# The second attention of a four-layer kernel, with scores made twice: by rows for the maximum, by columns less the maximum

## What is computed

```
# third layer, end of it:  y = ys + x * D_param ; x = x + y
def attention(x, ...):                       # fourth layer, 16 heads of 32
    kv_d = x @ kv_d_w ; q_d = x @ q_d_w
    k = concat(kv_d @ k_u_w, rope(x @ rope_k_w))
    q = concat(q_d @ q_u_w, rope(q_d @ rope_q_w))
    v = kv_d @ v_u_w
    scores = einsum('bqhd,bkhd->bhqk', q, k) / sqrt(32)
    scores = where(causal, scores, finfo.min)
    probs = softmax(scores)
    return einsum('bhqk,bkhd->bqhd', probs, v).reshape(b, s, H) @ o_w
```

## Time and profile before

| | us |
|---|---|
| median of 3 runs | 2087.54 |
| lowest and highest | 2086.83 and 2090.91 |
| the profiled execution | 2090.83 |
| its span, first to last instruction | 2089.1 |
| PE busy in the span | 1867.2 (89%) |
| DVE, ACT and POOL busy | 1369.4, 1000.2 and 801.1 |

### The profile page before, as it was taken

The page is one execution under the profiler, slowest core; times in us unless marked ns, Lnnn a source line. Parts: engine busy times, 40 slices in busy tenths (PEclk is TensorE's granted clock), DMA queues, the critical chain, the costliest instruction groups (busy, mean ns, idle before and its releaser), DMA issues. The chain is left out here.

```text
span 2089.1 us, 27327 instructions
## 1 busy us (share of the span) xinstructions
PE 1867.2 (89%) x9162; PEld 1222.5 (59%) x9162; DVE 1369.4 (66%) x2180; ACT 1000.2 (48%) x1743; POOL 801.1 (38%) x1073
## 2 busy tenths in 40 slices
PE   7978665899999899899999899899999999899795
PEld 3446444695448555596447656587447656588342
DVE  5765699475563699575654599676754599766311
ACT  1411675363422697363432598264242498365131
POOL 1146277442220277471220167381310157472301
PEclk9989855899999999999999999999999999999898
DMA  6336200000213175210213167210122158310693
GB/s 260 115 108 214 96 0 21 1 2 1 101 46 121 36 254 210 96 32 21 88 44 112 40 229 248 93 42 21 41 92 92 55 197 265 113 42 21 234 325 106
DMA packets 55065, 221.06 MB, mean 106 GB/s; under 512 B 6288, under 2 KB 6288, under 8 KB 46992
## 3 DMA queue, kind: packets, MB, share of 16 engines
q1 hardware_dynamic: 45776, 195.19, 26.9%
q0 software_dynamic: 5120, 16.78, 2.5%
q10 hardware_dynamic: 4032, 7.34, 1.0%
HBM read 179.70 MB, written 39.58 MB: 105 GB/s over the span
## 5 line engine op out<-in xcount | busy, mean ns | idle before, releaser
L2004 POOL TENSOR_TENSOR Y<-Y,HC 128x1024 f32<-128x1024 f32 x116 | 273.8, 2361 | 174.4 <-DVE HC L1378 173.7
L1367 DVE TENSOR_TENSOR_SCAN HS<-DA,ps 128x1024 f32<-128x1024 f32 x128 | 292.3, 2284 | 23.9 <-PE ps L761 13.5
L1748 ACT ACTIVATE DA<-DL,AB,AN 128x511 f32<-128x511 f32 x256 | 193.9, 807 | 14.7 <-DVE HS L1367 13.5
L544 PE MATMUL ps<-ring,XNT 128*128 128x512 f32 x384 | 176.1, 611 | 13.2 <-PEq L2036 9.1
L991 PE MATMUL ps<-ring,XBT 128*128 128x512 f32 x384 | 187.0, 593 | 0.2 <-ACT XBT L1427 0.2
L1867 ACT ACTIVATE PD<-ps,NMX 128x128 f32<-128x128 f32 (+3 forms) x256 | 134.9, 529 | 101.3 <-DVE NMX L1514 99.2
L1514 DVE TENSOR_REDUCE NMX<-ps 128x1 f32<-128x128 f32 (+3 forms) x256 | 124.3, 487 | 62.3 <-PE ps L829 61.9
L847 PE MATMUL ps<-V,PTD 128*128 128x33 f32 x1280 | 164.2, 262 | 0.0
L847 PEld LDWEIGHTS ps<-V,PTD 128*128 128x128 f32 x1280 | 162.6, 192 | 0.5 <-ACT PTD L869 0.5
L669 PE MATMUL ps<-XNH,tern 128*128 128x512 f32 x352 | 141.0, 401 | 10.8 <-DVE tern L1267 6.5
L1378 DVE TENSOR_TENSOR HC<-HS,ps 128x1024 f32<-128x1024 f32 x120 | 143.2, 1196 | 0.0
(11 more groups left out here) (251 smaller groups left out, 4015.4 us busy)
## 6 DMA issues: line engine op xcount, KB each, us to landing
ring<-experts_dram SPq DMA_DIRECT2D x48, 1024.0 KB, 5.2
tern<-tern_q SPq DMA_DIRECT2D x33, 768.0 KB, 4.3
ring<-experts_dram SPq DMA_DIRECT2D x48, 512.0 KB, 5.5
RAW<-tern_dram SPq DMA_DIRECT2D x22, 768.0 KB, 4.8
ring<-wqkv_dram SPq DMA_DIRECT2D x4, 3072.0 KB, 12.1
XB<-xg SPq DMA_DIRECT2D x42, 256.0 KB, 3.8
yg<-YB SPq DMA_DIRECT2D x42, 256.0 KB, 5.0
tern_q<-tern SPq DMA_DIRECT2D x11, 768.0 KB, 7.3
```

The costliest lines, as they stand in the source:

```text
L544: last = pe.matmul(ps[:, 2 + 3 * (i % 2) + part], XNT[:, k, tile(i)], wqkv[:, k, part * C:(part + 1) * C], start=(k == 0), stop=(k == NK - 1))
L1367: v.tensor_tensor_scan(HS[:, q].rearrange("p j t -> p (j t)"), DA[:, q].rearrange("p j t -> p (j t)"), ps[:, 2 * q:2 * q + 2].rearrange("p ...
L1748: s.activation(DA[:, u % 2, jj, 1:T], DL[:, j, 1:T], ACT.Exp, scale=AN[:, j * NS + n:j * NS + n + 1], bias=AB[:, j * NS + n:j * NS + n + 1 ...
L2004: p.tensor_tensor(y, y, HC[:, q], ALU.add).then_inc(c_y, 1)
```

## The change

Stage D is written anew in the manner of stage A. Per pair of heads there are three *units* (512, 512 and 256 columns for each of the two heads) and five kinds of PE work, in this order within a unit:

1. PV of an older pair (128 rows, 64 columns of the array),
2. masks: a bf16 identity times `mask_wide`, for the scores by rows (`pe_D_masks`),
3. spread: an f32r matrix of ones times DG, a diagonal matrix of the negative maxima, which puts minus the maximum of query q in column q of every partition (`pe_D_spread`),
4. rows: scores by rows, 32-row float32 matmuls added to the masks (`pe_D_rows`),
5. cols: scores by columns, 32-row float32 matmuls added to the spread (`pe_D_cols`).

So every score is made twice in float32: once by rows, from which DVE takes only the maximum (`v_D_max`, both heads in one instruction), and once by columns, less that maximum, which ACT exponentiates without a bias (`s_D_exp`). ACT also makes the diagonals, ten 128 x 128 products a pair (`s_D_diag`). POOL masks with `p_A_select` as in stage A. The loop has NP + 2 turns: turn t makes the rows of pair t, the columns of pair t - 1 and the PV of pair t - 2. PV writes always to bank 0, and PV of pair p waits for the division of pair p - 1 (`a_head`).

Gone are the stacks, the f32r split, QKS, the turning of PD, PTD and the turning of the heads; new are the 32 turns of QN into QT and KT at the front (`pe_qk` with "qk2"). The projection is made three quarters ahead (`pe_project_part`), the last quarter after the last division. On DVE a turn holds: the division of pair t - 3, the four maxima of pair t, then in turns 1 to 4 two `v_combine`, in turns 5 and 6 two `v_stats`, in turns 7 and 9 two `v_normalize`. On POOL all eight gathers go ahead of the first select.

At the end of stage C the last two HC are no longer added to Y; PE turns Y and HC one after the other into the same bank with float32 matmuls by the identity (32 matmuls for 16 transposes), and the experts' last matmuls are put around them. XS moves to where PT lies, so ACT waits in stage A, ahead of its second pair, for the scatter of XS. Buffers move accordingly.

The core of the diff:

```diff
-            for u in range(NU + 4):
-                if u < NU:
-                    ...
-                    pe.matmul(ps[:, bank, 0:(i + 1) * P], QKS[:, g % 2, hh, tile(i)],
-                              QKS[:, g % 2, GH + hh, 0:(i + 1) * P], start=True, stop=False, skip_group_check=True)
-                    pe.matmul(ps[:, bank, tile(i)], identb, mask_q, start=False, stop=True,
-                              skip_group_check=True).then_inc(d_scores, 1)
-                ...
+            for t in range(NP + 2):
+                rows, cols, heads = t < NP, 1 <= t <= NP, t >= 2
+                if t == NP + 1:
+                    pe.wait_ge(a_exp, 3 * (NP + t - 2) + 2)
+                    for i in range(2):
+                        pe_project_part(pe, i)
+                for unit in range(3):
+                    ...
+                    if heads:
+                        pe_D_pv(pe, t - 2, ((0,), (1,), (2, 3))[unit])
+                    if rows:
+                        pe_D_masks(pe, t, unit)
+                    if cols:
+                        pe_D_spread(pe, t - 1, unit)
+                    if rows:
+                        pe_D_rows(pe, t, unit)
+                    if cols:
+                        pe_D_cols(pe, t - 1, unit)
+        def pe_D_spread(pe, p, unit):
+            if unit == 0:
+                pe.wait_ge(d_diag, NT * (p + 1))
+                pe.wait_ge(d_max, max_count(p, 2))
+            ...
+        def pe_D_pv(pe, p, blocks):
+            if 0 in blocks:
+                if p == 0:
+                    pe.wait_ge(ones_a[1], 1)
+                pe.wait_ge(a_sel, NP + p + 1)
+                if p:
+                    pe.wait_ge(a_head, NP + p)
+            for kt in blocks:
+                last = pe_pv(pe, p, kt, 0)
+            if NT - 1 in blocks:
+                last.then_inc(a_pv, 1)
+            for t in range(NP + 3):
+                if t >= 3:
+                    v_pair(v, 1, t - 3)
+                if t < NP:
+                    for unit in range(3):
+                        v_D_max(v, t, unit)
+                if experts and 1 <= t <= NT:
+                    for n in (2 * t - 2, 2 * t - 1):
+                        v_combine(v, n)
+        def s_D_diag(s, p, unit):
+            for n, (i, _) in enumerate(D_ROWS[unit]):
+                s.wait_ge(d_max, NT * p + (0, 1, 3)[unit] + n + 1)
+                ...
+                for x in range(2):
+                    for block in ((i, i + 1) if i == NT - 1 else (i,)):
+                        ins = s.activation(DG[p % 2][:, x, tile(block)], ident, ACT.Copy,
+                                           scale=NMX[:, p % 2, i, x:x + 1])
-            v.tensor_tensor(Y[:, 2:4], Y[:, 2:4], HC[:, 1], ALU.add).then_inc(c_yt, 1)
-                    last = pe.transpose(ps[:, bank, tile(j)], Y[:, j, tile(i)], ident)
+                    pe.matmul(ps[:, bank, tile(j)], Y[:, j, tile(i)], ident, start=True, stop=False,
+                              skip_group_check=True)
+                    last = pe.matmul(ps[:, bank, tile(j)], HC[:, j // 2, j % 2, tile(i)], ident, start=False, stop=True,
+                                     skip_group_check=True)
```

## The result

The changed kernel takes 2320.1 us (median; 2316.6 to 2329.9), the kernel before 2089.2 us beside it: a ratio of 1.110, 95% interval 1.108 to 1.112. I had forecast 2270 with a range of 2195 to 2330. The sign was right, the wait that was added was the one named, and the time lies in the range; the middle was 50 us too low.

A forecast was written before the change was run, and what follows sets the result against it. PE's own work bounds stage D. The added wait for the division gives +29.6 us in the first step and +105.3 in the later three, the clock +47.6: +182.5 on 2087.5 makes 2270 us, range 2195 to 2330.

The forecast's parts named there:

- Rival 3: Stage D: PE never waits for the division; 2082 us, or 2024 at 8.6 us a pair; chance 0.04.
- PE's work for a pair: Stage D on PE: rows, columns, PV, masks and spread of one pair sum to 10.4 us, against 10.2 before.
- rows: 2.75 us; cols follow them: 2.25: Stage D on PE: a pair's row scores take 2.75 us with three group entries, then column scores 2.25.
- the 0.5 us of cover: Stage D: PE's last columns, 0.5 us, run during the division chain of 4.15 us, so a turn takes 14.1.
- twice my entries: Stage D on PE: doubling the charges for entering matmul groups (0.2 rows, 0.16 PV, 0.1 to 0.2 spread) gives 11.8 us a pair.
- E: Other DVE work between maximum and division: combines 1.5 us, stats 1.75 a turn; 9.2 a later step, 4.6 the first.
- its price: 1.7 us: Half clock after each PE gap in stage D costs 1.7 us; seven gaps in each of four steps, +47.6.
- Rival 2: Stage D: gaps lose twice the clock time (+48), or array-form entries cost twice the charge (+45); about 2316 us; chance 0.12.
- Rival 1: Stage D: the clock holds through the gaps, as dense work follows each; 2222 us; chance 0.18.
- -2 to +4 us a step: End of stage C: DVE's addition lost, 16 transposes become 32 float32 matmuls; bounds -2 to +4, taken as 0.
- my own sign of being wrong: Wrong if PV's wait is below 1 us, rows and cols far above 5, or stages A to C change over 5 a step.
- Rival 4: Stage D: two heads' scores not side by side, rows and cols 4.28 us each, +137; 2407 us; chance 0.04.

## Why the prediction was near, and where it failed

*The wait added, its releaser and its size: right.* PV stands 3.9 us for the division in the first step and 5.5 in later turns with entries (forecast 3.6 and up to 5.4), and 6.1 at the first pair of a later step, for the select (forecast 5.2). With two banks and the select in pieces it is gone from the turns. Rival 3 said that a free bank would be needed; it would not have been enough by itself, since the select came next, and with both the time was 2173.7 us and not 2024 to 2082, since PE then waited for the maxima and, in the later steps, for the first pair's select.

*PE's work for a pair: wrong, 8.7 us and not 10.4.* The failed step is "rows: 2.75 us; cols follow them: 2.25". The rows of a pair use two of the four groups of 32 rows of the array, the columns of the pair before the other two, and next to each other in the queue they run four side by side: 1.07, 1.09 and 0.65 us a unit, 2.8 instead of 5.0. The Trainium skill, TensorEngine Tiling (Array Packing), section Key Properties, says that tiles operate independently and that different ones can run matmuls in parallel. The trace of the change agrees with the page, with the 2.8 us. I had read the earlier trace rows for two and did not ask which rows the other pair uses. The other terms held: PV 2.6 forecast and measured, masks and spread 2.8 forecast, 3.3 measured with 0.24 of waiting in it. A turn at the full clock is thus 12.8 us where I had 14.1; as rows and columns now end together, the 0.5 us of cover that I subtracted isn't there. My bounds for a pair were added up wrongly too: by my own terms it is 8.7 us with nothing for any entry and 12.1 with twice my entries, where I wrote 8.6 and 11.8. That 8.7 was also measured is chance: the entries cost what I charged for PV, and it was the rows and columns that overlapped. E was right: 14.4 less 12.8, 1.6 us against my 1.5 to 1.75.

*The clock: right in kind, 80.7 us and not 47.6.* The failed step is "its price: 1.7 us", read from two gaps in the earlier trace rows which each had 3.4 us at 0.50 behind them; measured over the same 28 gaps it is 80.7 / 28 = 2.9 us. In the loop the low clock lasts 6.8 us a turn in the first step and up to 10.2 in the later ones, and once in the first and third step 20.5 us. Rival 2 had this mechanism (twice the 1.7 us, +48, 2316), and its time is the nearest to what was measured, but partly by luck: the clock took 33 us more than I forecast, not 48, and the rest came from elsewhere. Rival 1 (the clock holds) is wrong.

*The end of stage C: 23.6 us and not 0.* The failed step is the bound "-2 to +4 us a step". I had costed the turns of Y on PE and DVE's addition, and for these the 0 was right; I had not looked for what else of the change waits there. The ones of VA for the second attention are a new write on POOL, behind a wait for PE's last turn and ahead of the norms' RS, and POOL's queue was the one I did not read. By my own sign of being wrong, more than 5 us a step in the stages A to C, this shows: 4.2, 6.8, 5.8 and 6.8 us.

*Rival 4* (two heads not side by side) is excluded by the same rows.

The ledger against the measured +230: stage D without the clock +119.4 (530.9 less 411.5) where I had +134.9; the clock +80.7 for 47.6; the end of stage C +23.6 for 0; the rest, 7 us, lies at the front of stage D, 0.9 us a step, and in the clock of the stages outside. An error of -16 and errors of +33, +24 and +7 make the 48 by which the sum was short. The -16 is itself a balance: from the first PV to that of pair 6 a step took 8 us less than forecast (81.0 for 89.2 in the first), and what stands ahead of and behind these turns 3 to 5 us more. So the forecast was nearer than its terms: it owes some of that to errors of opposite sign.

## What to carry to other kernels

Where a wait stands in a loop, list everything that it waits for, and ask of each when it is complete: here one bank gave 66 us, the select 6, both together 146. On an engine that works in order, what is due first must stand first; four such orders (a write ahead of the norms, a division ahead of a maximum, gathers ahead of a select, the division whole instead of in halves) made up 98 of the 244 us between 2320.1 and 2076.1, and the bank and the select in pieces the other 146. And a gap costs its own length and what the clock takes behind it: to size the second, fill the gap with work that nobody reads.

## What the runs showed of the hardware

- Four 32-row float32 matmuls of two different kinds ran at once (450.05 to 451.12, 1.07 us for the rows of one pair and the columns of another) when they stood next to each other in the queue; with one f32r pair between them each kind took 1.1 us.
- Half the clock after a gap of 3.3 to 6 us did not last one fixed time: 3.4, 6.8, 10.2 and 20.5 us were all read in the stages D of the changed kernel. The same edit cost at most 34 us at a held clock and 111 without.
- A matmul into a bank that nothing reads, in 14 or 20 copies a turn, made the kernel 85 us faster (3.7%) without any other change.
- An ACT product of 128 x 128 with a column scale took 0.39 us, where I had estimated 0.3 from a DVE row of as many columns; ten of them a pair were covered.
